# A graph network layer on one core: the dst comparison of the binned groups made by VectorE instead of ScalarE

## The reference, cut to what matters

```
h0  = relu(layernorm(x))
row, col = src, dst                          # 206250 each
h = concat([h0[col], edge_attr])             # by dst
h = relu(h @ W1.T + b1)                      # 128 wide
h = relu(h @ W2.T + b2)
agg = segment_sum(h, row) / max(count, 1)    # by src
out = x + relu(concat([h0, agg, u]) @ Wa.T + ba) @ Wb.T + bb
```

## Time and profile before

| | us |
|---|---|
| median of 3 runs | 1901.95 (1894.68 to 1902.32) |
| the profiled execution | 1902.48 |
| its span, first to last instruction | 1900.7 |
| TensorE busy in the span | 1732.0 |
| VectorE busy | 1340.0, 4868 instructions |
| ScalarE busy | 1428.0, 2591 instructions |
| GpSimd busy | 1509.7, 991 instructions |

### The profile page before, as it was taken

One profiled execution on the slowest core, in us unless ns is written; L12 is line 12 of the kernel. 1 busy time (PEld: TensorE's weight loads), 2 busy tenths in 40 slices (PEclk: granted clock), 3 DMA queues, 4 the chain that ended last, 5 costly groups with the idle time before them and its releaser, 6 DMA issues.

```text
span 1900.7 us, 43131 instructions
## 1 busy us (share of the span) xinstructions
PE 1732.0 (91%) x12376; PEld 1463.0 (77%) x12376; DVE 1340.0 (71%) x4868; ACT 1428.0 (75%) x2591; POOL 1509.7 (79%) x991
## 2 busy tenths in 40 slices
PE   5898888999999999999899999999999999976828
PEld 3676777888888888888788888888888888866725
DVE  8665655777777777778677777777777777755727
ACT  4687877888888888888788888888888888842315
POOL 8488888888888888888888888888888888878850
PEclk9999999999999999999999999999999999988968
DMA  9988888999999999999899999999999999997755
GB/s 330 269 169 145 156 148 141 199 197 205 195 207 187 199 203 199 194 205 197 176 199 194 199 202 200 195 194 209 202 191 201 200 204 202 199 210 155 159 136 198
DMA packets 312201, 369.10 MB, mean 194 GB/s; under 512 B 40832, under 2 KB 196064, under 8 KB 311328
## 3 DMA queue, kind: packets, MB, share of 16 engines
q1 hardware_dynamic: 175200, 302.12, 55.1%
q0 software_dynamic: 135360, 62.15, 34.5%
q10 hardware_dynamic: 1408, 2.03, 0.3%
HBM read 203.87 MB, written 159.27 MB: 191 GB/s over the span
## 4 chain that ended last, share of the span: by engine, by line
POOL 53%; issue 20%; DMA 11%; PE 9%; ACT 3%; DVE 2%; SPq 1%; POOLq 0%; ACTq 0%; DVEq 0%
POOL sums L819 48%; DMA sums<-regA,idx 9%; POOL sums L807 5%; PE bank L1351 2%; PE bank L1400 2%; PE bank L1362 1%; DMA sums<-vscat,vidx 1%; PE bank L1374 1%; ACT h L921 1%; PE bank L1390 1%; ACT regA L929 1%; PE bank L1276 1%; PE bank L1476 1%; ACT regA L955 0%; DMA p_table<-regB 0%
## 5 line engine op out<-in xcount | busy, mean ns | idle before, releaser
L819 POOL DMA_INDIRECT sums<-regA,idx x844 | 1318.3, 1562 | 293.0 <-issue 242.6
L1351 PEld LDWEIGHTS bank<-h,regC 128*128 128x128 f32 x3072 | 387.4, 193 | 180.7 <-ACT h L940 127.8
L1351 PE MATMUL bank<-h,regC 128*128 128x130 f32 x3072 | 432.0, 284 | 64.5 <-ACT h L940 64.5
L1374 PE MATMUL bank<-regA,L 128*128 128x512 f32 x806 | 432.3, 619 | 2.8 <-DVE regA L1143 2.7
L1400 PE MATMUL bank<-w,h 128*128 128x128 f32 x3224 | 430.1, 277 | 0.0
L1400 PEld LDWEIGHTS bank<-w,h 128*128 128x128 f32 x3224 | 396.8, 194 | 1.1 <-ACT h L921 0.6
L921 ACT ACTIVATE h<-bank,b1c 128x512 f32<-128x512 f32 x403 | 275.6, 684 | 136.9 <-PE bank L1374 131.9
L1362 PE MATMUL bank<-regC 128*128 128x129 f32 x2352 | 296.9, 280 | 23.0 <-DVE regB L1130 12.7
L1390 PEld LDWEIGHTS bank<-h,regC 128*128 128x128 f32 x1688 | 218.9, 191 | 119.7 <-issue 91.3
L1362 PEld LDWEIGHTS bank<-regC 128*128 128x128 f32 x2352 | 277.4, 194 | 37.3 <-ACT vscat L961 21.9
L904 ACT ACTIVATE regC<-bank 128x520 f32<-128x520 f32 x384 | 231.8, 604 | 87.8 <-PE bank L1351 84.5
(11 more groups left out here) (143 smaller groups left out, 1526.9 us busy)
## 6 DMA issues: line engine op xcount, KB each, us to landing
regC<-slots SPq DMA_DIRECT2D x294, 260.0 KB, 5.6
regA<-in_ea SPq DMA_DIRECT2D x202, 256.0 KB
slots<-regC SPq DMA_DIRECT2D x192, 260.0 KB
src<-rows_src SPq DMA_DIRECT2D x107, 256.0 KB
slots<-regC SPq DMA_DIRECT2D x192, 138.1 KB
sums<-regA,idx POOLq DMA_INDIRECT x844
dstR<-rows_dst SPq DMA_DIRECT2D x101, 128.0 KB
sums<-zeros SPq DMA_DIRECT2D x20, 645.0 KB, 6.7
```

The source lines that it names most:

```text
L819: nc.gpsimd.indirect_dma_start(out=sums[k], out_offset=bass.IndirectOffsetOnAxis(ap=idx[:, n % RING, t:t + 1], axis=0), in_=scat[:, n % 4, ...
L1351: last = T.matmul(psSlot(t)[:, k, :], place, h2[:, g % 2, t, :], start=True, stop=True)
L1374: T.matmul(psL1(s % 2), L[:, s % RING, :], R[:, s % RING, :], start=True, stop=True).then_inc(l1_done, 1)
```

## The change

VectorE makes the one-hot half of every group, with the compare of L1143 and at the same place of its step, g = s + 1. ScalarE's two passes, their semaphores, the bias oh_bias and the VectorE instruction that made it are gone. For a binned group the compare now stands in VectorE's step just ahead of the rank reduction (L1150), and it is made one step later than ScalarE's passes were. TensorE and SyncE wait on oh_ready alone.

```diff
--- before
+++ after
@@ SyncE
                     if s % GPP == 0:
                         i = s // GPP
-                        wait(sp, oh_ready, sum(1 for g in range(GPP * (i - 1)) if not is_sorted(g)))
-                        wait(sp, oh_act_ready, sum(1 for g in range(GPP * (i - 1)) if is_sorted(g)))
+                        wait(sp, oh_ready, GPP * (i - 1))
@@ ScalarE
                 if is_sorted(s - 2):
                     evac_slots(s - 2, 1)
-                g = s + 2
-                if is_sorted(g):
-                    n, i = BINNED_NO[g], g // GPP
-                    if n == 0:
-                        act.wait_ge(oh_bias_ready, 1)
-                    act.wait_ge(dB_in[i % 2], 16 * (i // 2 + 1))
-                    wait(act, l1_done, g - RING + 1)
-                    nc.scalar.activation(R[D:P, g % RING, :], dB[D:P, i % 2, g % GPP, :], ACT.Abs, bias=oh_bias[D:P, :]).then_inc(oh_far, 1)
                 if 1 <= s and s + 1 < NG:
                     seed(s + 1)
-                if is_sorted(g):
-                    act.wait_ge(oh_far, n + 1)
-                    nc.scalar.activation(R[D:P, g % RING, :], R[D:P, g % RING, :], ACT.Relu, bias=1.0, scale=-1.0).then_inc(oh_act_ready, 1)
@@ VectorE
-            VE.tensor_scalar(oh_bias[:, :], oh_row[:, :], -1.0, None, ALU.mult).then_inc(oh_bias_ready, 1)
...
                 g = s + 1
-                if 0 <= g < NG and not is_sorted(g):
+                if 0 <= g < NG:
                     i = g // GPP
                     dve.wait_ge(dB_in[i % 2], 16 * (i // 2 + 1))
                     wait(dve, l1_done, g - RING + 1)
@@ TensorE
-                    pe.wait_ge(oh_ready, sum(1 for g in range(s + 1) if not is_sorted(g)))
-                    wait(pe, oh_act_ready, sum(1 for g in range(s + 1) if is_sorted(g)))
+                    pe.wait_ge(oh_ready, s + 1)
```

More of the change, by code:

```diff
@@ L342, in build @@
         oh_row = sb("oh_row", [P, 1], f32)
-        oh_bias = sb("oh_bias", [P, 1], f32)
         scrapc = sb("scrapc", [P, 1], f32)
@@ L440, in build @@
         oh_ready = sem("oh_ready")
-        oh_act_ready = sem("oh_act_ready")
-        oh_far = sem("oh_far")
-        oh_bias_ready = sem("oh_bias_ready")
         mask_ready = sem("mask_ready")
```

## The result

The changed kernel takes 1902.84 us in the median of 20 runs (1896.1 to 1906.09), the kernel before 1898.72 us in 20 runs (1893.1 to 1903.68). The ratio is 1.0021, 95% interval 1.0012 to 1.003: slower by about 4 us, within the 0.5% of the forecast and on the side to which its one price pointed (+2.8 us). The forecast's 1905 us lies 2 us over this because it counted from a profiled execution of 1902.48 us, 3.8 us over the median of 20; from that median the same step gives 1901.5.

A forecast was written before the change was run, and what follows sets the result against it. The prediction took GpSimd's own scatter stream as the bound. With 0 for all other terms and 2.8 us for the added comparisons, 1902.48 + 2.8 = 1905.3, so 1905 us, range 1895 to 1914.

The forecast's parts named there:

- GpSimd bounds the kernel, and the store hides both engines: GpSimd always scatters or pauses, 1.86 us each; 9 to 10 scatters lie ready, 17 to 19 us, hiding VectorE and ScalarE.
- VectorE's place: Added comparison at the head of VectorE's even steps, ahead of L1150, fits in idle time or cover: cost 0.
- SyncE and the start: SyncE's wait on one counter costs 0; first scatter stays at 69.6 us, at most 0.5 us either way.
- The price of the comparisons: 192 added VectorE comparisons, 102.0 us, delay GpSimd's scatters through the shared port: 15.5 x 102.0 / 571.6 = 2.8 us.
- the 15.5 us: Excess of GpSimd's mean scatter times over the 1.545 us median, summed over 844 and 96 scatters.
- cover of 0.44 us: Part of VectorE's 3.48 us addition at L1220 thought not to delay the scatter, which took 3.04 us too long.
- My upper end: Most that the added comparisons could cost GpSimd's scatters: 192 x 0.09 = 17 us.
- the first rival's weakened form: Each added comparison holds GpSimd's scatters back by 0.05 us or more, over 9.5 us in all; chance 0.10.
- ScalarE's relief: ScalarE loses 258.0 us of passes; GpSimd waited only 3.7 us for it, so gain 0, at most 3.7 us.
- The first in full: Added comparisons take GpSimd's time one for one, 192 x 0.531 = 102 us, giving 2004 us; chance 0.01.
- the third: TensorE sets the pace, so its 64.5 us of waits for ScalarE's h2 go: 1838 us; chance 0.05.
- The second: VectorE becomes the pace, 8.86 us a pair against GpSimd's 8.37: 77 us more, 1980 us; chance 0.03.

The follow-up runs named there:

- doubled: Changed kernel with each of VectorE's 403 comparisons made a second time right behind the first, into an unused buffer: ratio 1.0126 to the kernel before.
- apart run: Changed kernel with a second 64 x 512 comparison for 399 groups, placed away from the first, behind rank comparison or indices: ratio 1.0175 to the kernel before.
- the grid: Kernel before with no, 211 or 403 VectorE comparisons: with ScalarE's passes 0.9971, 1, 1.0011; without them 0.9990, 1.0014 and 1.0021 (changed kernel).
- long ones: Changed kernel with one added 64 x 2048 VectorE comparison for every four groups, 101 in all, into an unused buffer: ratio 1.0281 to the kernel before.
- after with the addition at the end: Changed kernel with VectorE's 3.48 us addition (L1220 of the kernel before) moved behind VectorE's loop: ratio 1.0024 to the kernel before.

## Why the prediction was right, point by point

**GpSimd bounds the kernel, and the store hides both engines.** Right for the change. The stream starts at 69.3 us and its last scatter starts at 1833.9 us, "issue" is its idle time, 10 to 11 scatters lie ready, and 0.96 us more of VectorE's work in a pair did not lengthen it. What the store did not cover when the rank comparison was made four times was the overflow scatter, whose lead I had not read: I counted indices of L1187 alone. And I had read the lead at 1000 and 1200 us only; in the doubled and the apart run it was used up at the end.

**VectorE's place.** Right: the idle time before L1150 and L1136 shrank from 389 to 234 us, and GpSimd's waits for indices did not grow.

**SyncE and the start.** Right: first scatter 0.3 us earlier, no new wait.

**The price of the comparisons**, 2.8 us by share of VectorE's time. Right in kind and near in size: 1.3 to 2.1 us by the grid, with intervals that reach from nothing to 4 us, and in the two traces the scatters took 1469.7 us for 1467.8, 2.6 us more without the one scatter under the long addition (3855 ns for 4575). The method was not as good as the number, and that it came so near is in part luck. First, the 15.5 us that I shared out hold 3.03 us of the addition, which is none of the three comparisons; without them the same sum gives 2.2 us. Second, the 0.05 to 0.09 us that one comparison could cost came from the misread cover of 0.44 us; with the 0.13 us that the runs show, a single one can cost more, as the 0.25 us at 922.03 above. Third, the price goes by where each comparison falls on a scatter, and a share of time can't know that: in the mean the old ones cost 22 to 26 ns, the new ones 7 to 11, doubled ones 41 in the scatters, apart ones 53, long ones 490. My upper end, 0.09 us each, would have held for the mean of all the short ones; the 0.05 us from which I counted the first rival's weakened form was passed by the apart ones and not by the change. The rule of the Trainium skill, SBUF — State Buffer, section "SBUF: two separate sides", an exclusive lock whose loser is blocked, agrees with the scatters that waited for VectorE's end and, the other way round, with the comparisons held to 0.78 us; it does not agree with those that cost a scatter nothing, and there the measurement decides.

**ScalarE's relief**, taken as 0 with 3.7 us of gain as its only end. This is the step that was off: it cost 1.9 to 3.6 us in three pairs of kernels, by means whose intervals are almost as wide. I had bounded it on one side only, since I saw no way in which less work could cost. Where the time goes stays open. The traces show the state that goes with it, ScalarE waiting for landed scatters 274, 296 and 329 us in the three kernels without passes and 62 to 67 in those with, but in single executions that differ by up to 5 us from their medians neither the scatters' durations nor GpSimd's waits grow with it. That a full store ties VectorE's work to the landing of scatters, and so to bad places, would fit and was not shown.

A second thing goes with relief and was not tested: the granted TensorE clock. In the mean of a run it was 0.960 to 0.969 in all executions of the four kernels without passes and without added work (after, after with the addition at the end, and the two of the grid), and 0.969 to 0.979 in the 77 of the kernel before whose clock is listed and in all of five variants that keep the passes. In the traces of the grid the difference lies ahead of the last scatter, where TensorE has the store between it and GpSimd (70 to 400 us: 0.95 and 0.96 for 0.97); behind the last scatter the clock is no lower without passes (0.80 to 0.83 for 0.76 to 0.84). How it could lengthen the kernel from there no run shows.

So the total came out at +4 us for +2.8 from two terms, of which I had one.

**The rivals.** The first in full and the third are excluded (TensorE's waits for h2 at the slot matmuls did not even fall: 76.0 us, and 64.5 in the earlier trace rows). The second exists at 2.89 us a pair and neither at 0.53 nor at the 0.96 of the rank comparison made twice; at the very end of the loop it shows already in the doubled and the apart run.

## What to carry to other kernels

Where one engine's stream is the bound and the others run ahead of it, count the lead of every kind of item in that stream, and at its end too, before you price work on the others: here the kind with the shortest lead starved. When work is moved to VectorE beside GpSimd's indirect DMAs, ask how long its single instructions from SBUF are and where they fall: a long one of 1.29 us cost up to 0.91 us in the places shown and 0.49 in the mean, a short one of 0.49 us cost 0.25 us in the place shown and 0.01 to 0.05 us in the mean. Only moving an instruction changes that too: the long addition held a scatter back by anything from 1.66 to 3.03 us. And a difference of 0.2% is not read off two traces: it took 20 runs of each and a grid of the change's halves, and the part of relief is still uncertain.

## What was not expected of the hardware

The price of one and the same VectorE instruction to a scatter under way ranged from nothing to 0.91 us, by its place alone, and the holding goes both ways (0.49 us became 0.78, 1.29 became 1.57). A scatter that starts under a VectorE comparison from SBUF, or under the long addition, is late by all of what is left of that instruction but 0.13 us. Making ScalarE's work smaller made the kernel slower by 0.10 to 0.19%, and adding 0.96 us to VectorE's pair made it faster by 0.17%; neither is explained.
